# Scatters of routed rows moved ahead of the second pair's normalisation factors on GpSimd

## The chip, the cores and the metric

One core of a Trainium2 chip runs the whole kernel. The metric is the device time of one execution in microseconds. A core has five engines with a queue each: PE (TensorE), DVE (VectorE), ACT (ScalarE), POOL (GpSimd) and SP (SyncE, which here only issues DMAs). Each engine works through its queue in order and waits on semaphores that the others raise.

## The reference

128 batches of 128 tokens with 256 features go through cross attention and then a routed feed-forward layer with 32 experts:

```python
x = x + xattn(layernorm(x), ctx, Wq, bq, Wk, bk, Wv, bv, Wo, bo)      # 16 heads of 16, softmax over 128 keys
# ffn, on layernorm(x):
logits = x_flat @ router_w.T + router_b
routed_idx = jnp.argmax(logits, axis=-1)
h = jax.nn.relu(x_flat @ w1 + b1)          # for each expert, 64 hidden
y = jax.nn.relu(h @ w2 + b2)
out_flat = y_all[routed_idx, jnp.arange(n)]  # each token takes its own expert
x = x + ffn
```

## The kernel before

A block is four batches (512 tokens); there are 32 blocks. The work is a software pipeline written out by hand: each engine has a loop over iterations s and, but for POOL, over the four batches u of block s, and each engine's order in the loop is its order on the chip. In iteration s the attention of block s runs, and beside it the projections of block s+1 and s+2, the second layer norm and the router's logits of block s-1, the choice and the ranks of block s-2, and the scatter of block s-3.

The steps that matter below:

- PE, batch u: the scores `sc` (L786), two transposes of a pair of normalised batches into `pA` (L748; in u = 0 and 1 of xn, in u = 2 and 3 of xn2), the transpose of the maxima (L779), attend of the batch before (L804, into `pB`), the subtraction of the maxima (L795), the scores for the next maxima (L773), a projection (L757), the values V (L764), and the output projection (L811). The scores of a batch wait for the copy of V of the batch before, and the transposes for the copy of the projection before.
- DVE, batch u: maxima (L574), residual (L583, which writes x2 into `row`), the copy mxT (L588), `xnT` (L593, in u = 0 and 1), then for the batch before `tr` (L598, behind attend), `inv`, `nrm` (L602), `aT`; then maxima again. In u = 0 also slot_sum (L637), in u = 1 best and choose (L614 to L626).
- ACT, batch u: the copy xnT (L441) or xn2T (L446), norm1 or norm2 (L428), the squares (L436), four exponentials (L452), the copy of V (L456), and the copy of the projection (L463 or, masked, twice L466).
- POOL, iteration s: rstd2(s-1, 0), place(s-3), rstd1(s+2), split(s+2), rstd2(s-1, 1), scatter(s-3), add_bo(s+1), meta(s-2), fresh_pages(s-2).

rstd2(q, h) makes the factors of the second layer norm for batches 2h and 2h+1 of block q with six operations on 128x2 values (L282 to L292); it waits for the squares of batch 2h+1, and norm2 of batch 2h waits for it. split (L306, L308) divides the context of a block into a high and a low part. scatter casts the four slots of each token to integers (L370) and issues four indirect DMAs (L374), one for a batch, which write 128 rows of 260 words each to the pages of their experts in HBM. It waits for the slots (slot_out), for the pages to have been filled, for the scatters of the block before, and for the token numbers (meta_out). add_bo (L298) adds the output bias to the x of the next block. SP loads x and a part of the context and fills a page behind each residual.

When all rows are scattered, SP loads the pages group by group, PE, ACT and DVE run each page through its expert, and POOL scatters the results to the output (L403).

Of the kernel before, what the change touches and what calls it, by code (L numbers as in the profile page):

```python
# [53 lines left out]
def build(nc, x, ctxT, wq, wk, wv, wo, bq, bk, bv, bo, wr, rb, w1, w2, consts, out):  # L54
# [14 lines left out]
    with ctx:  # L69
# [88 lines left out]
        def after(eng, name, per, q, k):  # L158
            eng.wait_ge(S[name], q * per + k + 1)
# [3 lines left out]
        def live(q):  # L163
            return 0 <= q < NQ
# [87 lines left out]
        def _(pool):  # L252
# [41 lines left out]
            def add_bo(q):  # L294
                if q == 0:
                    pool.wait_ge(S["bo_out"], 1)
                after(pool, "xn_out", 2, q, 1)
                pool.tensor_tensor(xs[:, q % 4], xs[:, q % 4], bo_s[:, :].unsqueeze(1).to_broadcast([P, QB, D]),  # L298
                                   ALU.add).then_inc(S["xb_out"], 1)

            def split(q):
                for c in range(2):
                    pool.wait_ge(S[f"ld_c{c}"], q * 16 + 16)
                if q >= 2:
                    after(pool, "V_done", 4, q - 2, 3)
                pool.tensor_copy(cHi[:, q % 2], cT[:, :, :]).then_inc(S["ctx_hi"], 1)  # L306
                after(pool, "ctx_hi", 1, q, 0)
                pool.tensor_tensor(cLo[:, q % 2], cT[:, :, :], cHi[:, q % 2].bitcast(F32), ALU.subtract).then_inc(S["ctx_out"], 1)  # L308
# [72 lines left out]
            for s in range(-1, NQ + 3):  # L381
                if live(s - 1):
                    rstd2(s - 1, 0)
                if live(s - 3):
                    place(s - 3)
                if live(s + 2):
                    rstd1(s + 2)
                if s >= 0 and live(s + 2):
                    split(s + 2)
                if live(s - 1):  # L390
                    rstd2(s - 1, 1)
                if live(s - 3):
                    scatter(s - 3)
                if live(s + 1):
                    add_bo(s + 1)
                if live(s - 2):
                    meta(s - 2)
                    fresh_pages(s - 2)
# [633 lines left out]
```

## Time and profile before

| | us |
|---|---|
| median of 3 runs | 1323.57 |
| lowest, highest | 1322.7, 1328.38 |
| the profiled execution | 1323.38 |
| its span, first to last instruction | 1321.3 |

Over the span PE is busy 87%, DVE 71%, POOL 65%, ACT 63%. Attention with its blocks reaches from the start to about 1016 us, the last choice and scatters to 1048, the pages to the end. In all tables a row of a timeline has the start in us from the span's start, the duration in us, the engine, the line, the operation, the tiles and their shape, a count where several in a row are merged, and in brackets how long the engine was idle before it and who released it. A start and a duration together give the end.

### The profile page before, as it was taken

Reading aid. Unit: us, or ns where it says so; the run is one execution under the profiler, and the core shown is the slowest. Engines: PE = TensorE matmul, PEld = TensorE weight load, DVE = VectorE, ACT = ScalarE, POOL = GpSimd, SP = SyncE. Lnnn points to the kernel's source line nnn. Section 1 sums busy time; section 2 is a strip of 40 time slices with the busy share of each in tenths; the row PEclk is TensorE's granted clock in tenths of the full one; section 3 lists DMA queues with packets and bytes.
Section 4 is the critical chain, followed back from the end, with each engine's and each line's share of the span. In section 5 each row is a group of like instructions: output and inputs, shape, how many; then the busy total and the mean of one; then the engine's idle time right before and its main releaser. Section 6 shows DMA issues by size and latency. Waiting matters only on the chain.

```text
span 1321.3 us, 38981 instructions
## 1 busy us (share of the span) xinstructions
PE 1146.4 (87%) x15015; PEld 877.5 (66%) x15015; DVE 941.1 (71%) x2449; ACT 832.5 (63%) x1892; POOL 854.2 (65%) x1613
## 2 busy tenths in 40 slices
PE   5999999999999999999999999999986087777775
PEld 4777777777777777777777777777764076666664
DVE  3788887788787888888778878788774155555554
ACT  3677776777777777777677777777763044444443
POOL 4535767767667777677776766777555656666555
PEclk8999999999999999999999999999998599999999
DMA  8315223422222222222222222221102245555540
GB/s 253 108 51 116 78 68 99 120 75 66 74 67 65 71 69 66 71 78 70 76 83 67 67 74 67 66 74 54 34 23 92 93 139 177 173 166 167 153 113 19
DMA packets 89235, 120.37 MB, mean 91 GB/s; under 512 B 12176, under 2 KB 71963, under 8 KB 88861
## 3 DMA queue, kind: packets, MB, share of 16 engines
q1 hardware_dynamic: 75230, 84.03, 22.5%
q0 software_dynamic: 13824, 33.85, 7.0%
q8 instruction: 122, 2.00, 0.7%
q14 instruction: 59, 0.48, 0.1%
HBM read 60.61 MB, written 59.31 MB: 91 GB/s over the span
## 4 chain that ended last, share of the span: by engine, by line
PE 53%; DVE 31%; issue 6%; ACT 4%; POOL 2%; DMA 1%; another core or an unknown queue 1%; DVEq 1%; SPq 0%; POOLq 0%; ACTq 0%
DVE mx L574 14%; PE pB L804 11%; PE pA L757 8%; PE pB L811 5%; PE sc L965 4%; PE sc L764 4%; PE m L973 3%; DVE tr L598 3%; PE sc L956 3%; PE sc L786 3%; DVE nrm L602 3%; PE m L773 3%; DVE row L583 3%; PE sc L795 2%; PE pA L748 2%
## 5 line engine op out<-in xcount | busy, mean ns | idle before, releaser
L574 DVE TENSOR_REDUCE mx<-m 128x4 bf16<-128x512 f32 x512 | 324.0, 673 | 53.3 <-PE m L773 53.0
L452 ACT ACTIVATE arena<-sc 128x512 f32<-128x512 f32 x512 | 264.5, 603 | 37.0 <-PE sc L795 23.1
L403 POOL DMA_INDIRECT out<-arena x160 | 159.7, 998 | 108.7 <-DVE arena L722 71.3
L786 PE MATMUL sc<-qk 32*128 32x256 f32 x2048 | 167.5, 397 | 0.3
L374 POOL DMA_INDIRECT pages<-row,slot_i x128 | 132.1, 1032 | 49.2 <-issue 32.2
L804 PE MATMUL pB<-arena 128*32 128x128 f32 x4096 | 147.7, 277 | 13.6 <-DVE row L583 0.5
L598 DVE STREAM_TRANSPOSE tr<-pB 128x512 f32<-128x512 f32 x128 | 91.8, 718 | 84.7 <-PE pB L804 74.2
L533 ACT ACTIVATE arena<-sc 128x256 f32<-128x256 f32 x160 | 61.3, 383 | 137.2 <-PE sc L956 87.2
L811 PE MATMUL pB<-wo_s,aT 128*128 128x256 f32 x512 | 138.6, 393 | 4.4 <-DVE aT L607 4.4
L804 PEld LDWEIGHTS pB<-arena 128*32 128x32 f32 x4096 | 108.6, 110 | 36.2 <-DVE row L583 30.9
L786 PEld LDWEIGHTS sc<-qk 32*128 32x128 f32 x2048 | 115.5, 186 | 0.7 <-ACT arena L456 0.6
L282 POOL TENSOR_SCALAR row<-row 128x2 f32<-128x2 f32 x64 | 14.6, 228 | 156.6 <-ACT xn L436 156.6
L773 PE MATMUL m<-qk 32*128 32x128 bf16 x2048 | 103.2, 217 | 2.8 <-ACT qk L466 1.8
L757 PE MATMUL pA<-cHi,wqkv 128*128 128x512 f32 x252 | 96.9, 425 | 9.4 <-DVE wqkv L641 9.4
L757 PE MATMUL pA<-xnT,wqkv 128*128 128x512 f32 x372 | 103.5, 414 | 0.0
L446 ACT ACTIVATE xn2T<-pA 128x512 f32<-128x512 f32 x64 | 38.2, 597 | 103.6 <-remote 61.7
L965 PE MATMUL sc<-arena,cT 128*128 128x128 f32 x640 | 101.0, 282 | 0.0
L811 PEld LDWEIGHTS pB<-wo_s,aT 128*128 128x128 f32 x512 | 87.6, 190 | 18.3 <-issue 5.9
L764 PE MATMUL sc<-wqkv,cHi 128*128 128x256 f32 x512 | 97.9, 284 | 0.5 <-ACT arena L452 0.5
L764 PEld LDWEIGHTS sc<-wqkv,cHi 128*128 128x128 f32 x512 | 87.9, 190 | 11.4 <-ACT arena L452 0.6
L973 PE MATMUL m<-w2s,arena 128*128 x160 | 53.8, 419 | 46.8 <-ACT arena L537 33.1
L773 PEld LDWEIGHTS m<-qk 32*128 32x128 bf16 x2048 | 63.1, 93 | 46.3 <-issue 32.3
(145 smaller groups left out, 2717.4 us busy)
## 6 DMA issues: line engine op xcount, KB each, us to landing
arena<-pages SPq DMA_DIRECT2D x40, 520.0 KB
cT<-ctxT SPq DMA_DIRECT2D x64, 256.0 KB, 4.2
xs<-x_in SPq DMA_DIRECT2D x128, 128.0 KB, 2.1
pages<-empty SPq DMA_DIRECT2D x120, 130.0 KB, 3.0
pages<-empty SPq DMA_DIRECT2D x1, 5200.0 KB, 19.3
out<-arena POOLq DMA_INDIRECT x160
w2s<-w SPq DMA_DIRECT2D x1, 2080.0 KB
qk<-w SPq DMA_DIRECT2D x1, 2064.0 KB
```

The source lines that it names most:

```text
L374: pool.indirect_dma_start(pages, bass.IndirectOffsetOnAxis(slot_i[:, u:u + 1], 0), row[:, q % 4, u, :], None, bounds_check=last_slot, oob_ ...
L403: pool.indirect_dma_start(out_rows, bass.IndirectOffsetOnAxis(pr[:, r, COL_TOKEN:COL_TOKEN + 1].bitcast(U32), 0), pr[:, r, 0:D], None, bou ...
L452: act.activation(pt[:, u % 2, g].rearrange("p i k -> p (i k)"), sc[g][:, :], ACT.Exp).then_inc(S["exp_out"], 1)
L574: ins = dve.tensor_reduce(mx[:, 32 * g:32 * g + 4], mb[i][:, :].rearrange("p (h k) -> p h k", h=4), AX.X, ALU.max)
L598: dve.transpose(tr[:, :], pB[:, :]).then_inc(S["tr_out"], 1)
L757: ins = pe.matmul(proj_bank(q, n)[:, :], wqkv[:, w, a, i, c * P:(c + 1) * P], src[:, i, :], start=(i == 0 and (a, b) == HI_LO[0]), stop=(i ...
L764: ins = pe.matmul(sc[0][:, 0:D], (cHi, cLo)[a][:, q % 2, i, u * P:(u + 1) * P], wqkv[:, 2, b, i, :], start=(i == 0 and (a, b) == HI_LO[0]) ...
L773: ins = pe.matmul(mb[i][:, j * P:(j + 1) * P], qMh[rows, q % 2, m, c, u * P:(u + 1) * P], kTh[rows, q % 2, c, u * P:(u + 1) * P], start=Tr ...
L786: pe.matmul(dst, kT[rows, q % 2, c, u * P:(u + 1) * P], qM[rows, q % 2, :, c, u * P:(u + 1) * P], start=(c == 0), stop=False, skip_group_c ...
L804: ins = pe.matmul(pB[32 * g:32 * g + 32, j * P:(j + 1) * P], vs[:, q % 2, u, h, :], pt[:, u % 2, g, j, :], start=True, stop=True)
L811: ins = pe.matmul(pB[:, 0:D], aT[:, i, :], wo_s[:, i, :], start=(i == 0), stop=(i == 1))
L965: ins = pe.matmul(sc[2 + n % 2][:, 0:P], w1p[:, n % W1R, i * HID:i * HID + P], pnT[:, n % DEEP, i * P:(i + 1) * P], start=(i == 0), stop=( ...
```

## The change

In POOL's loop scatter(s-3) now stands ahead of rstd2(s-1, 1), directly behind split(s+2).

```diff
                 if s >= 0 and live(s + 2):
                     split(s + 2)
+                if live(s - 3):
+                    scatter(s - 3)
                 if live(s - 1):
                     rstd2(s - 1, 1)
-                if live(s - 3):
-                    scatter(s - 3)
                 if live(s + 1):
                     add_bo(s + 1)
```

PE, DVE, ACT and SP have the same instructions in the same order. POOL has the same instructions. In the middle of the run, POOL's queue stood so, from the split to add_bo; what is in brackets is what a row waits for:

```order
L308 TENSOR_TENSOR cLo<-cT,cHi 128x1024 [waits ctx_hi]
L282 TENSOR_SCALAR row<-row 128x2 [waits sq_out]
L283 TENSOR_SCALAR row<-row 128x2
L285 TENSOR_TENSOR sq<-row 128x2 [waits mean2_out]
L288 TENSOR_TENSOR row<-row,sq 128x2 [waits eps2_out,sq2_out]
L290 TENSOR_TENSOR row<-row,half 128x2 [waits var2_out]
L292 TENSOR_TENSOR row<-row 128x2 [waits pow2_out]
L370 CAST slot_i<-slot 128x4 [waits slot_out,scattered,fill0]
L374 DMA pages<-row,slot_i 20480x260 [waits meta_out,slot_int]
L374 DMA pages<-row,slot_i 20480x260 x3
L298 TENSOR_TENSOR xs<-xs,bo_s 128x1024 [waits xn_out]
```

At the same place it now reads:

```order
L308 TENSOR_TENSOR cLo<-cT,cHi 128x1024 [waits ctx_hi]
L370 CAST slot_i<-slot 128x4 [waits slot_out,scattered,fill0]
L374 DMA pages<-row,slot_i 20480x260 [waits meta_out,slot_int]
L374 DMA pages<-row,slot_i 20480x260 x3
L282 TENSOR_SCALAR row<-row 128x2 [waits sq_out]
L283 TENSOR_SCALAR row<-row 128x2
L285 TENSOR_TENSOR sq<-row 128x2 [waits mean2_out]
L288 TENSOR_TENSOR row<-row,sq 128x2 [waits eps2_out,sq2_out]
L290 TENSOR_TENSOR row<-row,half 128x2 [waits var2_out]
L292 TENSOR_TENSOR row<-row 128x2 [waits pow2_out]
L298 TENSOR_TENSOR xs<-xs,bo_s 128x1024 [waits xn_out]
```

The cast and the four scatters have passed the six operations of rstd2, whose wait for the squares (sq_out) now stands behind them.

In iteration 32 there is no split and no add_bo. On POOL, from the end of place to meta, it was:

```order
L360 TENSOR_TENSOR nxt<-nxt,shift_d 128x32 [waits nxt_old,shift_out]
L282 TENSOR_SCALAR row<-row 128x2 [waits sq_out]
L283 TENSOR_SCALAR row<-row 128x2
L285 TENSOR_TENSOR sq<-row 128x2 [waits mean2_out]
L288 TENSOR_TENSOR row<-row,sq 128x2 [waits eps2_out,sq2_out]
L290 TENSOR_TENSOR row<-row,half 128x2 [waits var2_out]
L292 TENSOR_TENSOR row<-row 128x2 [waits pow2_out]
L370 CAST slot_i<-slot 128x4 [waits slot_out,scattered,fill1]
L374 DMA pages<-row,slot_i 20480x260 [waits meta_out,slot_int]
L374 DMA pages<-row,slot_i 20480x260 x3
L315 TENSOR_SCALAR expert<-idx 128x4 [waits idx_out]
```

And it now is:

```order
L360 TENSOR_TENSOR nxt<-nxt,shift_d 128x32 [waits nxt_old,shift_out]
L370 CAST slot_i<-slot 128x4 [waits slot_out,scattered,fill1]
L374 DMA pages<-row,slot_i 20480x260 [waits meta_out,slot_int]
L374 DMA pages<-row,slot_i 20480x260 x3
L282 TENSOR_SCALAR row<-row 128x2 [waits sq_out]
L283 TENSOR_SCALAR row<-row 128x2
L285 TENSOR_TENSOR sq<-row 128x2 [waits mean2_out]
L288 TENSOR_TENSOR row<-row,sq 128x2 [waits eps2_out,sq2_out]
L290 TENSOR_TENSOR row<-row,half 128x2 [waits var2_out]
L292 TENSOR_TENSOR row<-row 128x2 [waits pow2_out]
L315 TENSOR_SCALAR expert<-idx 128x4 [waits idx_out]
```

The scatters stand directly behind place here, and rstd2 of the last block behind them.

## Rows read from the trace of the kernel before

**Rows 1.** The page's chain of work that ended last, share by engine.

```profile
PE 53%; DVE 31%; issue 6%; ACT 4%; POOL 2%; DMA 1%; another core or an unknown queue 1%; DVEq 1%; SPq 0%; POOLq 0%; ACTq 0%
```

**Rows 2.** Waits (total us, times, longest), and L602 (ns min/median/max).

```profile
POOL row L282 <- ACT xn L436: 156.6, 64, 9.5
...
ACT xn2T L446 <- remote: 61.7, 23, 2.7
...
L602 DVE TENSOR_TENSOR nrm<-tr,inv x128: 424/441/1610, 43.7 to 1012.6; 128x256 f32<-128x256 f32 x128
```

**Rows 3.** Timeline of POOL in block 19 and at the start of block 20's factors.

```profile
617.60 2.37 POOL L308 TENSOR_TENSOR cLo<-cT,cHi 128x1024 fp32r<-128x1024 f32 x1
622.36 0.23 POOL L282 TENSOR_SCALAR row<-row 128x2 f32<-128x2 f32 x1 [2.40 <-ACT xn L436]
...
624.27 0.20 POOL L292 TENSOR_TENSOR row<-row 128x2 f32<-128x2 f32 x1
...
625.11 1.13 POOL L374 DMA_INDIRECT pages<-row,slot_i  x1 [0.51 <-POOL slot_i L370]
...
630.19 2.40 POOL L298 TENSOR_TENSOR xs<-xs,bo_s 128x1024 f32<-128x1024 f32 x1
...
652.97 0.23 POOL L282 TENSOR_SCALAR row<-row 128x2 f32<-128x2 f32 x1 [2.21 <-ACT xn L436]
```

**Rows 4.** Timeline of DVE in batches 1 and 2 of block 19.

```profile
622.13 0.72 DVE L598 STREAM_TRANSPOSE tr<-pB 128x512 f32<-128x512 f32 x1
...
627.87 0.41 DVE L583 SCALAR_TENSOR_TENSOR row<-pB,xs 128x256 f32<-128x256 f32 x1
...
629.38 0.22 DVE L588 COPY mxT<-m 128x128 bf16<-128x128 bf16 x1 [1.09 <-PE m L779]
631.04 0.72 DVE L598 STREAM_TRANSPOSE tr<-pB 128x512 f32<-128x512 f32 x1 [1.44 <-PE pB L804]
...
632.08 0.80 DVE L602 TENSOR_TENSOR nrm<-tr,inv 128x256 f32<-128x256 f32 x1
```

**Rows 5.** Timeline of ACT in the same stretch.

```profile
624.95 0.38 ACT L456 ACTIVATE arena<-sc 128x256 f32<-128x256 f32 x1 [0.47 <-PE sc L764]
625.23 1.44 ACT L466 ACTIVATE qk<-pA,bqm,cst 128x512 f32<-128x512 f32 x2
629.34 0.60 ACT L446 ACTIVATE xn2T<-pA 128x512 f32<-128x512 f32 x1 [2.67 <-remote]
629.84 0.59 ACT L428 ACTIVATE xn<-row 128x256 f32<-128x256 f32 x1
```

**Rows 6.** Timeline of PE in the same stretch.

```profile
620.98 1.08 PE L804 MATMUL pB<-arena 128*32 128x128 f32 x32
...
626.96 0.66 PE L748 MATMUL pA<-cst,xn 128*128 128x128 f32 x4
...
628.34 1.40 PE L804 MATMUL pB<-arena 128*32 128x128 f32 x32
```

**Rows 7.** DVE's copy mxT of batch 0 in blocks 1 and 2.

```profile
62.79 0.23 DVE L588 COPY mxT<-m 128x128 bf16<-128x128 bf16 x1
...
91.77 0.23 DVE L588 COPY mxT<-m 128x128 bf16<-128x128 bf16 x1
```

**Rows 8.** Timelines of POOL, PE and DVE in batch 2 of block 4.

```profile
165.89 1.13 POOL L374 DMA_INDIRECT pages<-row,slot_i  x1 [0.83 <-POOL slot_i L370]
...
168.79 1.08 PE L804 MATMUL pB<-arena 128*32 128x128 f32 x32
...
171.81 0.72 DVE L598 STREAM_TRANSPOSE tr<-pB 128x512 f32<-128x512 f32 x1 [2.15 <-remote]
```

**Rows 9.** Timelines of DVE and POOL in iteration 32.

```profile
1013.45 0.24 DVE L637 TENSOR_REDUCE slot<-t 128x4 f32<-128x128 f32 x1
...
1015.81 0.31 POOL L282 TENSOR_SCALAR row<-row 128x2 f32<-128x2 f32 x1 [3.85 <-ACT xn L436]
...
1022.70 0.97 POOL L374 DMA_INDIRECT pages<-row,slot_i  x1 [0.30 <-issue]
```

## The prediction

> **What bounds the kernel now.** I read the chain of work first: PE has 53% of it, DVE 31%, POOL 2% [rows 1]. POOL is no engine on which time is lost directly, so four scatters begun earlier, or six tiny operations begun later, are worth nothing by themselves. The question is what they do to PE, DVE and ACT. Next I read the waits of the whole run [rows 2]. POOL's largest is the first operation of rstd2 (L282) behind ACT's squares, 156.6 us in 64 times: that is the gap the change fills. Another is odd: ACT's xn2T copy waited 23 times, 61.7 us in total, for a releaser that the trace can't name (`remote`). To see what lies behind it I opened one steady block, 613.9 to 644.5 us; its period is 30.61 us (622.36 to 652.97, the same instruction one block on) [rows 3].
>
> In that block the scatters start at 625.11 (call this t0), and add_bo behind the fourth at 630.19 [rows 3]. What PE finishes in this time is signalled late. The transposes of xn2 start at 626.96 and take 0.66, so they end at 627.62 [rows 6], but ACT's copy of them starts only at 629.34, after 2.67 idle [rows 5]. DVE is done with the residual at 628.28 and should copy mxT at once; it does so at 629.38 [rows 4]. Attend (L804) starts at 628.34, takes 1.40 where batch 1's took 1.08 [rows 6], and `tr` behind it starts at 631.04 [rows 4]. So there are two holds: completions due at t0+2.5 come out at t0+4.2, and those due at t0+4.6 at t0+5.9. In batch 1, with no scatter running, `tr` starts at 622.13 without idle, 0.07 after attend's end at 622.06 [rows 4, 6]. DVE's `nrm` (L602) then takes 0.80, where its median is 0.44, beside add_bo's last 0.5 us [rows 2 to 4].
>
> I take the holds to belong to the scatters: they recur at the same distance in the steady blocks, and the one block with batches in full swing and no routing work ran in 28.98 us (62.79 to 91.77) [rows 7]. What inside the chip joins a scatter to PE's signals no row says.
>
> **What the change does, part by part.** The instructions and their counts are the same; only POOL's order moves.
>
> 1. The scatters. cLo ends at 619.97. From rstd2's end (624.47) to t0 was 0.64, so t0 becomes 619.97 + 0.64 = 620.61, 4.5 us earlier [rows 3]. slot_out, the one late input, is DVE's slot_sum just behind batch 0, so it isn't late. Carried along, the holds cover 623.1 to 624.8 and (from 625.2 at the latest) to 626.5. DVE works in that time without needing PE: after `tr` at 622.13 [rows 4] come the maxima, best and choose, and the residual at 627.87, whose input PE makes soon behind V. ACT needs V at 624.95 and then runs the two masked projections from 625.23 to 626.67, and had 2.67 idle behind them [rows 5].
>    The doubtful completion is that of V, due about 624.9, t0+4.3. If it is let through, ACT loses nothing, mxT follows at 628.28, attend runs 628.34 to 629.42 and `tr` starts at 629.45, 1.59 earlier. `nrm` loses its extra 0.36 too, since add_bo is over by then. Both together are 1.95, but a block that is otherwise free took 28.98, so I cap the gain at 30.61 - 28.98 = 1.6. If V is caught in the second hold, it comes at t0+5.93 = 626.54; the copy and the projections end 0.28 + 1.44 later, at 628.3; the transposes start 0.29 behind (as 626.96 behind 626.67) and take 0.66, to 629.2; attend ends 1.1 later, and `tr` starts at 630.35, 0.7 earlier. For being caught speaks block 4: scatters from 165.89, attend ended at 169.87, t0+3.98, and `tr` started only at 171.81, t0+5.92 [rows 8]. Against it: the first hold lets go at t0+4.2, just before V is due. The rows are equally near to both, so I take the middle, 1.15 per block.
> 2. rstd2's second half (the factors of batches 2 and 3). It took 622.36 to 624.47, 2.11. It now stands behind the four scatters, 5.08 from t0 to add_bo [rows 3]: 625.7 to 627.8. Who waits is ACT's norm2 of batch 2, which stands behind the xn2T copy. Freed of its hold that copy starts at 627.65, and norm2 0.5 later, 628.15 (as 629.84 behind 629.34 [rows 5]). The margin is 0.35, and behind norm2 stand only the squares before the exponentials, which cannot start before attend's end at 629.42 and the subtraction behind it; two ACT steps of 0.5 lie between, so the real margin is about 0.5 to 1.0. Cost: nothing, between 0 and 0.5 per block if the scatters are slowed by more than that margin.
> 3. add_bo and meta. add_bo starts at 627.8 instead of 630.19; the expert is chosen before the residual at 627.87, and POOL then waits for the ranks as before. It may slow the residual at 627.87, which reads one operand of SBUF: at most the 0.36 that `nrm` loses now. I take 0, and the cap of 1.6 covers it.
> 4. Loads. SP issues x, fill and half of the context behind the residual, at 621 as at 628. All four scatters now run beside the earlier set instead of two beside the later. No engine waited for these loads in the steady block; the cost by itself is 0, but it can lengthen the holds (rival C).
> 5. The end. In iteration 32 POOL idled 3.85 before rstd2 at 1015.81, though the slots were summed at 1013.69 [rows 9]. The scatters now fill that from 1013.8. By the steady block's lengths, 0.7 + 5.08 + 2.27, rstd2 ends at 1021.85 instead of the scatters' end at 1023.70: 1.9 earlier, on the path, since POOL alone leads from there to the pages.
>
> The sum: 29 blocks (3 to 31) scatter beside attention. 29 x 1.15 = 33.4, and 1.9 at the end: 35.3. The profiled execution took 1323.38 (span 1321.3 and 2.1 around it), practically the median 1323.57, so no correction: 1323.4 - 35.3 = **1288**. Its own range, from 0.7 to 1.6 per block, is 1301 to 1275.
>
> The Trainium skill bears on this against me. "SBUF — State Buffer", section "Who interferes with whom", says that only the port pair shared by VectorE and GpSimd causes contention and that TensorE waits for nobody there. The trace agrees for `nrm` beside add_bo (0.80 us against a median of 0.44). For PE it shows late completions beside the scatters, which that rule doesn't give; if the rule is the whole story, the holds belong to something else and rival B is what happens.
>
> **The rivals.**
> B, the holds stay where they are, since they belong to batch 2 of a block (its PE work or SP's loads behind it) and not to the scatters. For: I infer the link from position, and no row names a releaser. Against: the loads are issued behind every second batch, but PE is late only here. Then only `nrm` is freed, at most 29 x 0.36 = 10, and the end, 1.9: 1311 to 1321.
> C, **slower**: the holds begin earlier than the rows of before can show, because the first scatter now meets batch 1's attend. That attend is due at 622.06, t0+1.45, and DVE takes it up with no slack. If it is held as the first group is, to t0+4.2 = 624.8, DVE loses 2.7; less the 1.6 that goes away, that is 1.1 per block, 32 in all, less 1.9: 1353. It decides from where a completion at t0+1.45 is caught. Against: no wait in the rows shows a completion held that was due before t0+2.5. For: before, nothing on which an engine waited fell due between 1.0 and 2.5, so the rows are silent there, and the loads are now at hand.
> D, the price is paid in other coin: longer holds, scatters slowed by DVE's SBUF work, norm2 late. With 0.7 to 1.2 per block of it little is left: 1316 to 1332.
> E, the change doesn't do what it says: slot_out or the previous scatters hold slot_i back. Slots are summed in batch 0 and the last scatters were issued a block before, so I give this nothing of its own.
>
> **How the numbers follow.** Forecast (1275 to 1301) 0.50; B 0.15; C 0.14; D 0.16; better than 1275 0.05. Within 0.5% (6.6 us, about what a measurement of this kernel can tell from no change) are 1317 to 1330. Faster: 0.50 + 0.05 + two thirds of B (0.10) = 0.65. Same: the rest of B and most of D, 0.18. Slower: C and the tail of D, 0.17. The range of 8 in 10 leaves out C and a little at the low end: 1272 to 1332.
>
> **What would show it.** Scatters at 4.5 us before their present distance to the block's start; ACT's `remote` wait for xn2T gone or under 15 us in total; DVE's mxT copy following the residual within 0.1, and `tr` some 1.0 behind it instead of 1.44 behind a late start; a period of 29.0 to 29.9. V's copy on ACT starting at once means the upper gain, 1.6 us late the lower. Wrong would be: a wait before batch 1's `tr` (C), the same waits at batch 2 (B), norm2 waiting for POOL (D).

## The result, and the profile after

The changed kernel takes 1419.19 us (median of 4 runs, 1413.83 to 1427.14) against 1324.78 us of the kernel before (4 runs, 1322.7 to 1328.38). The ratio is 1.069, with a 95% interval from 1.064 to 1.074: the change makes the kernel 7% slower, where 3% faster was forecast. The profiled execution took 1421.39 us, its span 1418.3.

A hold, in what follows, is a completion of TensorE (the semaphore update by which it tells the others that a result is there) that comes late. First, where in the program the time went. These two groups hold all of a block's scatters and all copies `mxT`; the numbers behind the counts are the shortest, the median and the longest in ns, then the starts of the first and the last in us. Before:

```profile
L374 POOL DMA_INDIRECT pages<-row,slot_i x128: 971/982/1251, 134.9 to 1046.7; - x128
L588 DVE COPY mxT<-m x128: 223/225/226, 35.9 to 1005.7; 128x128 bf16<-128x128 bf16 x128
```

After:

```profile
L374 POOL DMA_INDIRECT pages<-row,slot_i x128: 971/976/1255, 129.6 to 1146.4; - x128
L588 DVE COPY mxT<-m x128: 224/225/226, 35.4 to 1107.0; 128x128 bf16<-128x128 bf16 x128
```

The last copy `mxT` comes 101.3 us later, so the whole loss lies in the attention blocks. From that copy to the last scatter it is 39.4 us instead of 41.0, the only place where the change did what it was meant to do; the pages behind take 2.7 less, which no run explains.

To see in which batch the time goes I take the starts of `mxT`, of which every batch has one. Over the blocks 4 to 29, a block (from one batch 0 to the next) takes 30.62 us before and 34.29 after. By batches:

| us, mean of blocks 4 to 29 | 0 to 1 | 1 to 2 | 2 to 3 | 3 to next | block |
|---|---|---|---|---|---|
| before | 6.98 | 8.45 | 7.56 | 7.63 | 30.62 |
| after | 6.98 | 11.72 | 7.99 | 7.60 | 34.29 |

The step from batch 1 to batch 2 is where the scatters now lie. The page's line of the chain that ended last, and the longest waits of the run that are new or have grown (total us, times, longest; the first was 34.7 us before, the last 9.8):

```profile
PE 52%; DVE 26%; issue 8%; another core or an unknown queue 5%; ACT 3%; POOL 2%; DVEq 1%; DMA 1%; SPq 0%; POOLq 0%; ACTq 0%
```

```profile
POOL need L327 <- ACT rks L484: 192.1, 31, 8.7
ACT arena L452 <- remote: 105.6, 28, 4.0
...
DVE tr L598 <- remote: 72.9, 22, 4.1
```

Before, 1% of the chain was put down to an unknown releaser [rows 1]; now it is 5%. ACT's xn2T wait for `remote` [rows 2] is gone, as forecast. In its place ACT waits for it 28 times ahead of the exponentials (L452), 3.8 us each time, and DVE 22 times ahead of `tr`, 3.3 us each.

Block 19 again, in the same stretch as [rows 3 to 6]. It now starts at 672.8. POOL, the first and the fourth scatter and the bias:

```profile
679.28 1.14 POOL L374 DMA_INDIRECT pages<-row,slot_i  x1 [0.29 <-POOL slot_i L370]
...
683.28 0.97 POOL L374 DMA_INDIRECT pages<-row,slot_i  x1 [0.30 <-issue]
...
686.32 2.38 POOL L298 TENSOR_TENSOR xs<-xs,bo_s 128x1024 f32<-128x1024 f32 x1
```

PE and ACT (attend of batch 1, the scores for the next maxima, the projection, the exponentials):

```profile
679.87 1.08 PE L804 MATMUL pB<-arena 128*32 128x128 f32 x32
...
682.07 0.30 PE L773 MATMUL m<-qk 32*128 32x128 bf16 x4 [0.48 <-issue]
...
683.02 1.64 PE L757 MATMUL pA<-xnT,wqkv 128*128 128x512 f32 x6
```

```profile
685.13 2.06 ACT L452 ACTIVATE arena<-sc 128x512 f32<-128x512 f32 x4 [3.96 <-remote]
```

DVE:

```profile
684.35 0.72 DVE L598 STREAM_TRANSPOSE tr<-pB 128x512 f32<-128x512 f32 x1 [3.34 <-remote]
...
687.70 1.14 DVE L615 TENSOR_TENSOR eq<-lg,top 128x128 f32<-128x128 f32 x1
...
691.35 0.23 DVE L588 COPY mxT<-m 128x128 bf16<-128x128 bf16 x1
692.57 0.72 DVE L598 STREAM_TRANSPOSE tr<-pB 128x512 f32<-128x512 f32 x1 [0.99 <-PE pB L804]
```

Call the first scatter's start t0, 679.28. Attend ends at 680.95, t0+1.67, but `tr` starts only at t0+5.07; the exponentials start at t0+5.85. Batch 2 is now undisturbed: `mxT` follows the residual at once and `tr` 1.22 after it, as forecast. So the holds did move with the scatters, and at their new place they catch attend and the subtraction of the maxima, on which both DVE and ACT wait. PE goes on to its next work meanwhile, but slowly: the projection starts 3.15 behind attend's start, where it was 1.56 in the kernel before. Since the ends of matmuls in a trace are modelled, the rows don't say whether a late completion was sent late or came late.

From `tr` to `mxT` DVE then works almost without a break (0.24 us idle on average over the 26 blocks), so it is `tr`, and what DVE meets behind it, that make the step from batch 1 to 2. The exponentials' wait is beside that path.

And DVE meets something: there is a second loss in these rows. DVE's comparison `eq` (L615) takes 1.14 beside POOL's bias, add_bo (L298), which now directly follows the factors. Over the run, before:

```profile
L615 DVE TENSOR_TENSOR eq<-lg,top x32: 291/293/1474, 103.3 to 1030.1; 128x128 f32<-128x128 f32 x32
```

After:

```profile
L615 DVE TENSOR_TENSOR eq<-lg,top x32: 291/1440/2180, 102.8 to 1129.8; 128x128 f32<-128x128 f32 x32
```

The two are tied. `eq` ends when add_bo does, 0.14 behind it in block 19. In the 26 blocks `tr` starts anywhere from t0+4.3 to 5.8; where it starts early `eq` takes 2.0 us, where it starts late 0.64, and the step stays between 11.5 and 11.8. So in the changed kernel the end of add_bo fixes the step, and DVE meets add_bo only because the hold has made it late.

And a third. The step from batch 2 to 3 takes 7.25 us in 14 of the 26 blocks, as in block 19, and 8.6 to 10.2 in the others, as in block 18. These are stretches of the trace after (stretch, length, PE busy and instructions, granted clock, DMA share, GB/s), the first two of block 18 and the last two of block 19:

```profile
652.50:656.20 3.70, 2.00 (x30) 1.00 0.00 0
656.20:658.70 2.50, 2.39 (x55) 0.65 0.34 107
...
687.50:691.10 3.60, 2.04 (x30) 1.00 0.00 0
691.10:693.60 2.50, 2.39 (x60) 1.00 0.38 110
```

PE, standing behind `eq` and the maxima, was busy for 2.00 of 3.70 us, and then the granted clock was 0.65 for a while (a mixture of the two levels, 2.4 and 1.2 GHz); in block 19, after nearly the same pause, it stayed at 1.00. A fall costs 1.5 us in most of these blocks. The kernel before shows no lowered clock in its blocks 4 to 29.

### The profile page after: what moved, and what is told of

Read it like the earlier page. It is cut to its first block, busy times and chain, and to the rows that moved or that the text cites. A ratio compares the mean times of both kernels' runs of the same rounds, so it can differ in the third digit from the quotient of the medians.

```text
span 1418.3 us, 38981 instructions
## 1 busy us (share of the span) xinstructions
PE 1174.7 (83%) x15015; PEld 887.1 (63%) x15015; DVE 963.3 (68%) x2449; ACT 830.2 (59%) x1892; POOL 855.9 (60%) x1613
## 3 DMA queue, kind: packets, MB, share of 16 engines
q0 software_dynamic: 13824, 33.85, 6.5%
## 4 chain that ended last, share of the span: by engine, by line
PE 52%; DVE 26%; issue 8%; another core or an unknown queue 5%; ACT 3%; POOL 2%; DVEq 1%; DMA 1%; SPq 0%; POOLq 0%; ACTq 0%
PE pA L757 11%; DVE mx L574 11%; PE pB L804 8%; PE pB L811 7%; PE sc L764 5%; PE m L773 4%; PE sc L965 3%; DVE eq L615 3%; PE sc L795 3%; PE m L973 3%; PE sc L786 2%; DVE row L583 2%; PE sc L956 2%; DVE tr L598 2%
## 5 line engine op out<-in xcount | busy, mean ns | idle before, releaser
L452 ACT ACTIVATE arena<-sc 128x512 f32<-128x512 f32 x512 | 264.6, 603 | 159.8 <-remote 105.6
L773 PE MATMUL m<-qk 32*128 32x128 bf16 x2048 | 115.8, 221 | 27.6 <-issue 24.2
L533 ACT ACTIVATE arena<-sc 128x256 f32<-128x256 f32 x160 | 61.2, 382 | 130.8 <-PE sc L956 76.4
L764 PE MATMUL sc<-wqkv,cHi 128*128 128x256 f32 x512 | 102.7, 294 | 28.3 <-ACT arena L452 27.7
L327 POOL TENSOR_TENSOR need<-rks,room 128x32 f32<-128x32 f32 x32 | 8.1, 253 | 192.1 <-ACT rks L484 192.1
L773 PEld LDWEIGHTS m<-qk 32*128 32x128 bf16 x2048 | 68.9, 95 | 79.4 <-issue 65.9
L757 PE MATMUL pA<-xnT,wqkv 128*128 128x512 f32 x372 | 113.7, 444 | 0.0
L456 ACT ACTIVATE arena<-sc 128x256 f32<-128x256 f32 x128 | 50.0, 390 | 71.4 <-PE sc L764 71.4
```

Of the source, the lines that this page charges most:

```text
L452: act.activation(pt[:, u % 2, g].rearrange("p i k -> p (i k)"), sc[g][:, :], ACT.Exp).then_inc(S["exp_out"], 1)
L757: ins = pe.matmul(proj_bank(q, n)[:, :], wqkv[:, w, a, i, c * P:(c + 1) * P], src[:, i, :], start=(i == 0 and (a, b) == HI_LO[0]), stop=(i ...
L764: ins = pe.matmul(sc[0][:, 0:D], (cHi, cLo)[a][:, q % 2, i, u * P:(u + 1) * P], wqkv[:, 2, b, i, :], start=(i == 0 and (a, b) == HI_LO[0]) ...
L773: ins = pe.matmul(mb[i][:, j * P:(j + 1) * P], qMh[rows, q % 2, m, c, u * P:(u + 1) * P], kTh[rows, q % 2, c, u * P:(u + 1) * P], start=Tr ...
```

## The experiments

e1 to e5 leave out rows, so only their blocks, measured as above, can be compared; the others do all the work and are compared by the time of the whole run too. "Before" is the kernel before on the same chip beside the run. Where no interval is given, there was one run. The steps are means of one trace.

| run | us | before | ratio (95%) | 1 to 2 | 2 to 3 | block |
|---|---|---|---|---|---|---|
| e1, before, no scatters | 1293.5 | 1311.1 | | 8.86 | 7.41 | 30.86 |
| e2, after, no scatters | 1290.6 | 1311.1 | | 8.51 | 7.60 | 30.69 |
| e3, after, rows skipped | 1266.1 | 1311.1 | | 7.37 | 7.25 | 29.23 |
| e4, after, one scatter | 1298.0 | 1311.1 | | 8.66 | 7.54 | 30.78 |
| e5, after, two scatters | 1318.7 | 1328.0 | | 8.98 | 7.25 | 30.82 |
| e6, after, scatters wait | 1318.9 | 1328.0 | | 8.09 | 7.81 | 30.51 |
| e7, before, behind the bias | 1421.3 | 1328.0 | | 8.52 | 10.96 | 34.09 |
| e8, scatters apart | 1416.9 | 1328.0 | 1.067 (1.064 to 1.071) | 10.38 | 8.92 | 34.13 |
| e9, after, loads wait | 1446.4 | 1318.7 | 1.096 (1.094 to 1.099) | 11.75 | 8.94 | 35.30 |
| e10, before, loads wait | 1318.6 | 1318.7 | 0.999 (0.998 to 1.000) | 8.45 | 7.67 | 30.73 |
| e11, apart, bias late | 1293.8 | 1318.7 | 0.981 (0.978 to 0.983) | 7.36 | 7.61 | 29.74 |
| e12, after, bias late | 1359.0 | 1321.1 | 1.028 (1.025 to 1.032) | 10.33 | 7.24 | 32.16 |
| e13, all apart | 1276.9 | 1321.1 | 0.968 (0.965 to 0.972) | 7.36 | 7.24 | 29.19 |
| e14, first one early, apart | 1290.5 | 1321.1 | 0.977 (0.974 to 0.981) | 7.35 | 7.60 | 29.72 |

### e1 to e4: is it the scatters, and what of them?

e1 and e2 take the scatters out of the kernel before and of the changed one; a store to a spare word counts for them.

```
-                for u in range(QB):
+                for u in range(0):
...
+                pool.memset(gone[:, :], 0.0).then_inc(S["scattered"], 64)
```

> The kernel before with its 128 scatters to the pages left out; a memset of one column raises their semaphore, so no routed row is written and the pages hold only the fill. Theory 1 (a run of scatters holds back PE's completions, and that is what both kernels pay): the holds in batch 2 vanish, the period falls from 30.6 to about 29.0 us, and with the tail shorter by three groups of scatters (some 15 us) the time is about 1265. Rival (the holds belong to batch 2 of a block, its loads or PE's own work): the period stays at 30.6 or falls only by 0.4, time about 1300 to 1310.

> The changed kernel with the scatters left out in the same way. Theory 1: its order costs nothing by itself, so it takes what the run before it takes within 5 us. Rival (the later factors or add_bo beside other work of DVE cost the time): it stays well above that run, by up to the 95 us that the change cost, and DVE's or ACT's waits of the changed kernel in batch 1 are still there.

e3 keeps the four instructions but gives them slots beyond the last page:

```
-                pool.tensor_copy(slot_i[:, :], slot[:, :]).then_inc(S["slot_int"], 1)
+                pool.tensor_scalar(slot_i[:, :], slot[:, :], 1048576.0, None, ALU.add).then_inc(S["slot_int"], 1)
```

> The changed kernel with slots beyond the end of the pages, so that POOL still makes all four scatters but their rows are out of bounds and none is written. If making the scatter on POOL is what holds PE back, the holds and the 1419 us stay. If the moving of the rows is (512 rows of 1040 bytes per block), the holds go and the time is about that of the changed kernel without scatters plus the length of POOL's tail, some 1285.

e4 issues one of the four, at the first one's place (`range(1)` for `range(QB)`, and the counts waited for to match).

> The changed kernel with one of the four scatters of a block (rows of batches 1 to 3 are not scattered), at the place of the first. If each scatter holds PE for a time of its own, the attend of batch 1, due 1.67 us behind the scatter's start, is still held, by 1 to 2 us, and the period is 30 to 31 us. If only scatters in a run do it (a second one begun while the first moves its rows), nothing is held and the period is about 29.0.

In e1, e2 and e4 no engine waits ahead of batch 1's `tr`, yet they gain nothing over before in the step 1 to 2. The reason is `eq`, 1.78, 1.44 and 1.59 us long on average in blocks 4 to 29, here in e1 (POOL's add_bo is at L299 and `eq` at L617 there):

```profile
622.59 2.36 POOL L299 TENSOR_TENSOR xs<-xs,bo_s 128x1024 f32<-128x1024 f32 x1
```

```profile
623.32 1.78 DVE L617 TENSOR_TENSOR eq<-lg,top 128x128 f32<-128x128 f32 x1
```

Without scatters between the factors and add_bo, add_bo runs beside `eq`, and `eq` lasts until 0.15 us behind add_bo's end. No expectation had that, so the 29.0 us a block of e1 and e4 did not come; that e2 would be within 5 us of e1 did. e3 has the scatters' time on POOL, so that add_bo comes at 604.57, behind `eq`; all holds are gone as well, and with 29.23 us a block and 1266 us in all it is faster than the 1285 expected. The page's line of the queue, and DVE in block 19:

```profile
q0 software_dynamic: 13824, 0.17, 0.7%
```

```profile
598.77 0.72 DVE L598 STREAM_TRANSPOSE tr<-pB 128x512 f32<-128x512 f32 x1
...
602.11 0.29 DVE L615 TENSOR_TENSOR eq<-lg,top 128x128 f32<-128x128 f32 x1
```

The queue shows as many packets as before, but 0.17 MB for 33.85, and in block 19 `tr` starts without idle. POOL's scatter instructions are there, about as long as before, and hold nothing, so the hold needs rows that are really written. That it is the moving itself is not shown: in e13, below, a hold is over before the first packet of its rows. And `eq` takes 0.29 in each of the 26 blocks: with the changed order and no hold, DVE is past `eq` before add_bo starts.

29.2 us is what a block takes when nothing disturbs it; the kernel before is 1.4 above that. e4 has a single scatter and no hold; it is the block's first one, and the experiments below show that this matters.

### e5: two scatters

As e4, with two of the four.

> The changed kernel with the first two of a block's four scatters only; half of the routed rows are therefore never written, and only the attention blocks can be compared (changed kernel 34.3 us a block there, with one scatter 30.8, with none 30.7). Theory 1, the rows in flight hold back the completions of TensorE, and the more the longer: one scatter of 128 rows holds nothing for long, four hold attend's completion for 3.4 us; two should hold it for about half of that, 1 to 1.7 us, so 31.5 to 32.5 us a block. Theory 2, there is a threshold on what the queue can hold: two are either as harmless as one (30.8) or as bad as four (34.3). Theory 3, it is the first scatter's place beside attend that matters and one scatter was enough of it: 30.8.

`tr` and the exponentials of batch 1; the first scatter is at 622.89:

```profile
625.81 0.72 DVE L598 STREAM_TRANSPOSE tr<-pB 128x512 f32<-128x512 f32 x1 [1.19 <-PE pB L804]
```

```profile
625.89 2.07 ACT L452 ACTIVATE arena<-sc 128x512 f32<-128x512 f32 x4 [1.11 <-PE sc L795]
```

Both are let go at t0+2.9 to 3.0. With one there was no wait, with four `tr` came at t0+5.07. The hold grows with the number of scatters in the run. The block's time hides it: 30.82 us is what the second and third theory said, because `eq`, met later, is shorter here (0.73 on average where e4 has 1.59). By the rows it is the first theory's hold of 1 to 1.7.

### e6 and e7: the four together at two other places

e6 adds a wait ahead of the scatters of the changed order:

```
                 if live(s - 3):
+                    if live(s - 1):
+                        after(pool, "sq_out", 4, s - 1, 3)
                     scatter(s - 3)
```

> The changed kernel's order on GpSimd, all four scatters, but the first waits until ScalarE has squared batch 3, some 2.3 us later than in the changed kernel and some 2 us earlier than in the kernel before. The hold should move with it. Theory 1, what is held is whatever TensorE completes while the rows are moved: attend of batch 1 would then post before the rows (no wait of 3.3 us ahead of tr in that batch) and the wait moves to the next completions, as score maxima or projection; a block of 31.5 to 33.5 us, since GpSimd's own later work (factors, residual bias) comes 2.3 us later too. Theory 2, the changed order itself costs (factors behind the scatters, bias beside the eq comparison) and not the time of the rows: 34.3 us or more.

e7 puts them one place later than before:

```
                 if live(s - 1):
                     rstd2(s - 1, 1)
+                if live(s + 1):
+                    add_bo(s + 1)
                 if live(s - 3):
                     scatter(s - 3)
-                if live(s + 1):
-                    add_bo(s + 1)
```

> The kernel before with the four scatters moved one place the other way, behind the addition of the residual bias (2.4 us later). Nothing is left out. Theory 1, the holds move 2.4 us later: the two of the kernel before (ahead of tr and of the copy of maxima in batch 2) go, and others come at attend and maxima of the end of batch 2 or of batch 3; the block stays between 30 and 34 us according to where DVE waits. Also the bias, now straight behind the factors, runs beside the eq comparison, as in the runs without scatters, and costs some 1.2 us in batch 1. Theory 2, only an earlier place is harmful: 30.6 plus that 1.2 us.

e6 begins the scatters at 619.37 in block 19, 9.1 into the block (6.5 after, 11.2 before), and costs no more than the kernel before; its block is shorter than either theory said. ACT's xn2T copy is held until 625.26, t0+5.9, but DVE waits little. Its `nrm` at 626.88 took 2.23, beside add_bo. In e7 the hold lies on attend and subtraction again, of batch 2 this time, with t0 at 680.53:

```profile
686.28 0.72 DVE L598 STREAM_TRANSPOSE tr<-pB 128x512 f32<-128x512 f32 x1 [3.36 <-remote]
```

```profile
686.36 2.06 ACT L452 ACTIVATE arena<-sc 128x512 f32<-128x512 f32 x4 [3.11 <-remote]
```

They come at t0+5.75 and t0+5.83. The block is nearly as long as the changed kernel's, but that is chance. Against an undisturbed block (e13), e7 loses 1.16 us in the step 1 to 2, again with `eq` beside add_bo (1.46 us), and 3.72 in the step 2 to 3. There `tr` starts 2.4 later behind `mxT`, and the other 1.3 come behind it, in a step in which the granted clock is lower in all 26 blocks (0.69 on average). In block 19 (PE, PEld, DVE, ACT and POOL busy, granted clock, DMA share, GB/s):

```profile
682.68:693.70 11.02, 10.17 (x109) 7.70 (x109) 5.73 (x17) 5.19 (x12) 5.35 (x14) 0.69 0.29 86
```

So earlier or later is not the point: moved 4.7 us ahead (the change) or 2.1 behind (e7), the hold of the four catches an attend and the subtraction near its start; at the two places between (e6 and the kernel before) it catches them near its end or not at all.

### e8: one at a time

The scatters are issued singly: behind the factors, the bias, the expert's work and the list of fresh pages.

`scatter` is split into the making of `slot_i` and `scatter_one(q, us)`, which issues those of the batches us. Against the kernel before:

```
                 if live(s - 3):
                     scatter(s - 3)
+                if live(s - 3):
+                    scatter_one(s - 3, (0,))
                 if live(s + 1):
                     add_bo(s + 1)
+                if live(s - 3):
+                    scatter_one(s - 3, (1,))
                 if live(s - 2):
                     meta(s - 2)
+                if live(s - 3):
+                    scatter_one(s - 3, (2,))
...
```

> Nothing is left out. The four scatters of a block are issued one at a time, between the factors, the bias, the expert's work and the list of fresh pages, so that at least 2 us lie between two of them. Theory 1, one scatter alone holds nothing that is waited for (the run with one of four: 30.8 us a block against 30.7 without any), and only a run of them does: 29.5 to 30.8 us a block, 1290 to 1320 us in all against 1324.8 of the kernel before. Theory 2, what counts is the number of rows and not their spacing: each scatter holds a completion for about 1 us, four times a block, 31 to 34 us a block, 1330 to 1420 us.

By its time this seemed to speak for "each scatter costs by its rows". The rows say otherwise: of batch 1's and 2's `tr` none waits longer than the 0.99 that it waits in an undisturbed block. Batch 3's does, behind the fourth scatter, which begins 9.6 us behind the third:

```profile
693.80 1.08 POOL L376 DMA_INDIRECT pages<-row,slot_i  x1 [0.17 <-issue]
...
695.24 0.72 DVE L609 STREAM_TRANSPOSE tr<-pB 128x512 f32<-128x512 f32 x1 [1.46 <-PE pB L815]
```

Attend's matmuls end at 694.67, 0.87 behind the scatter's start, and `tr` starts 0.57 later. So a scatter by itself can hold PE too, for half a microsecond here; the step from batch 3 to the next takes 7.85 us (7.79 in e11 and e14, which have their fourth scatter there as well) instead of 7.61. The great loss is another one. What went wrong is `eq`, with add_bo next behind a scatter:

```profile
678.61 1.12 POOL L376 DMA_INDIRECT pages<-row,slot_i  x1 [0.51 <-POOL slot_i L370]
679.77 2.35 POOL L298 TENSOR_TENSOR xs<-xs,bo_s 128x1024 f32<-128x1024 f32 x1
```

```profile
678.99 3.29 DVE L626 TENSOR_TENSOR eq<-lg,top 128x128 f32<-128x128 f32 x1
```

PE then stood, and its clock fell (same columns as above):

```profile
681.10:684.50 3.40, 0.02 (x1) 1.00 0.11 39
...
686.50:689.50 3.00, 3.00 (x12) 0.50 0.56 167
```

These two steps take 19.3 us (10.38 + 8.92), 4.7 more than e3's 14.6. 3.0 of them are `eq`; most of the rest is the clock: the six projections that come next, first in e8, then in e3, where the clock stayed up:

```profile
686.55 2.93 PE L768 MATMUL pA<-xnT,wqkv 128*128 128x512 f32 x6
```

```profile
599.19 1.66 PE L757 MATMUL pA<-xnT,wqkv 128*128 128x512 f32 x6
```

### e9 and e10: are SyncE's loads part of it?

In the changed kernel three loads (x, a fill, half a context) are issued 0.6 to 1.4 us behind the first scatter. e9 makes them wait until the scatters have landed:

```
+                    if u == 3 and q >= 2:
+                        sp.wait_ge(S["scattered"], 64 * (q - 1))
                     if live(q + 4):
                         load_x(q + 4, u)
```

> The changed kernel, nothing left out; only SyncE's loads that fell among the scatters (fourth rows of x, one page fill, half a context; issued 0.6 to 1.4 us after the first scatter's start) now wait until the block's scatters have landed. Theory 1, the rows of the scatters and those loads share the DMA engines, and it is the two together that hold TensorE's completions for 3.4 us: with the loads gone the hold is 1 to 2 us long, as the first one of the kernel before (1.7 us, no load near it), and a block takes 31.5 to 32.5 us instead of 34.3. Theory 2, the rows alone do it, whatever else is moved: 34 us or more.

e10 does the same to the loads behind batch 0's residual in the kernel before (`u == 0 and q >= 3`, `64 * (q - 2)`).

> The kernel before, nothing left out; the loads that SyncE issues at the scatters' end (first rows of x, one fill, half a context; 3.2 to 4.1 us after the first scatter's start) wait until the block's scatters have landed. Theory 1 (rows and loads together hold): the second hold, 1.3 us ahead of tr in batch 2, goes, 0.8 to 1.3 us less a block, 1290 to 1305 us in all; the first one, with no load near it, stays. Theory 2 (rows alone): both stay, 1320 to 1330 us.

The holds stay in both, so the loads are not their cause. In e9, t0 at 692.28:

```profile
696.59 0.72 DVE L600 STREAM_TRANSPOSE tr<-pB 128x512 f32<-128x512 f32 x1 [2.59 <-remote]
...
699.93 2.18 DVE L617 TENSOR_TENSOR eq<-lg,top 128x128 f32<-128x128 f32 x1
...
704.61 0.23 DVE L590 COPY mxT<-m 128x128 bf16<-128x128 bf16 x1
```

But in the changed kernel they lengthen the hold. Over the blocks 4 to 29 `tr` starts at t0+4.22 on average instead of t0+5.05, and the exponentials at t0+5.09 instead of 5.83 (block 19, with t0+5.8, is one of four of the 26 in which they come as late as that). The first theory was right in that, though not in its 1 to 2 us. It gains nothing, because `eq` starts sooner behind add_bo's start (699.60) and lasts 2.18 in most blocks, 0.83 longer than in the changed kernel: just what `tr` had won. That e9 is slower still, by 1.0 us a block, comes from the clock, which falls more often (8.94 in the step 2 to 3 instead of 7.99). In e10 nothing changes: `tr` of batch 2 still waits 1.42 us.

### e11, e13, e14: apart, with the bias out of the way

e11 is e8 with the expert's work (which waits for `idx`, made from `eq`) ahead of add_bo, and a wait ahead of the third scatter. Against the kernel before:

```
                 if live(s - 3):
                     scatter(s - 3)
+                    scatter_one(s - 3, (0,))
+                if live(s - 2):
+                    meta(s - 2)
                 if live(s + 1):
                     add_bo(s + 1)
+                if live(s - 3):
+                    scatter_one(s - 3, (1,))
+                    if live(s):
+                        after(pool, "sq_out", 4, s, 0)
+                    scatter_one(s - 3, (2,))
                 if live(s - 2):
-                    meta(s - 2)
                     fresh_pages(s - 2)
+                if live(s - 3):
+                    scatter_one(s - 3, (3,))
```

> Nothing left out. The scatters of a block one at a time again, but the residual bias is no longer next behind the first of them: it comes behind the expert's work, which waits for the comparison (eq) that the bias held up for 3.0 us in the run before; the third scatter also waits for ScalarE's square of batch 0. Theory 1 (single scatters hold nothing; the 34.1 us a block of the run with them apart came from the bias holding eq, and from the lower granted clock after TensorE had stood): eq takes 0.3 us again, 29.3 to 30.6 us a block, 1285 to 1320 us in all. Theory 2 (each scatter costs by its rows): over 31.5 us a block, over 1345 us.

1293.8 us: faster than before by 1.7 to 2.2%. `eq` is 0.29 in block 19. The second and third scatter are still 1.39 apart, and the maxima of that time wait for a releaser that the trace can't name:

```profile
616.55 1.09 POOL L376 DMA_INDIRECT pages<-row,slot_i  x1 [0.17 <-issue]
617.94 0.98 POOL L376 DMA_INDIRECT pages<-row,slot_i  x1 [0.30 <-issue]
```

```profile
618.61 1.29 DVE L585 TENSOR_REDUCE mx<-m 128x4 bf16<-128x512 f32 x2 [0.42 <-remote]
```

e13 parts those two as well, with `after(pool, "max_out", 8, s, 7)` for the wait on `sq_out`.

> Nothing left out. As the run with the scatters apart and the bias late (29.7 us a block), but the third scatter waits for the last maxima of batch 3, so that it no longer follows 1.4 us behind the second; that pair held score maxima's completion for 1.9 us. Theory 1 (only scatters that follow one another within some 1.4 us hold anything): the two holds behind the pair go, 29.2 to 29.6 us a block, 1275 to 1292 us. Theory 2 (each scatter's rows hold what comes meanwhile): a hold appears wherever the third scatter goes, 29.7 us a block or more, 1294 us or more.

```profile
600.84 1.13 POOL L376 DMA_INDIRECT pages<-row,slot_i  x1 [0.51 <-POOL slot_i L370]
...
605.53 1.09 POOL L376 DMA_INDIRECT pages<-row,slot_i  x1 [0.17 <-issue]
611.17 0.99 POOL L376 DMA_INDIRECT pages<-row,slot_i  x1 [4.56 <-DVE mx L585]
615.18 1.08 POOL L376 DMA_INDIRECT pages<-row,slot_i  x1 [0.16 <-issue]
```

With at least 4 us from one to the next, a block takes 29.19 us, as much as in e3, which moves no rows. 1276.9 us is 3.2% faster than before and the best version found: the same scatters with the same rows, apart and at these places, cost nothing.

That is not the same as holding nothing. The trace also keeps the moment of each semaphore's update. In block 19 PE's scores for the next maxima end at 605.71, 0.18 behind the second scatter's start, and their update comes at 606.85, 1.14 late. It is so in all 26 blocks; completions due 0.6 behind the fourth scatter come 0.67 late, and attend, due 1.2 behind the third, 0.25. DVE and ACT are busy with earlier work just then, so almost nothing waits. The second scatter's first row packet starts only at 607.24, behind the hold. Nothing is late behind a block's first scatter, in e13 (due 0.7 and 1.0 behind it) or in e4 (0.4, 0.5 and 1.7). Why the first differs stays open.

e14 is e11 with the first scatter alone at the place that the change gave to all four.

> Nothing left out. As the run with the scatters apart and the bias late, with the first scatter alone moved ahead of the second pair's factors, to the place that the change gave it, 1.5 us ahead of attend's end. Theory 1 (it is the run of four that was harmful, not the early place): no wait ahead of tr in batch 1, 29.5 to 30.0 us a block, 1285 to 1300 us. Theory 2 (a scatter ahead of attend holds it): a wait of 1 us or more ahead of tr in batch 1, 30.7 us a block or more, over 1315 us.

```profile
606.62 1.13 POOL L376 DMA_INDIRECT pages<-row,slot_i  x1 [0.29 <-POOL slot_i L370]
```

```profile
608.16 0.72 DVE L609 STREAM_TRANSPOSE tr<-pB 128x512 f32<-128x512 f32 x1
```

`tr` starts without idle, 1.54 behind the scatter's start. The early place is harmless for the block's first scatter alone; the run of four was not. Whether one of the other three would be harmless there no run shows.

### e12: the change without the collision

The changed kernel, its four scatters in a run where the change puts them, with only add_bo moved behind the expert's work:

```
+                if live(s - 2):
+                    meta(s - 2)
                 if live(s + 1):
                     add_bo(s + 1)
                 if live(s - 2):
-                    meta(s - 2)
                     fresh_pages(s - 2)
```

> The changed kernel, nothing left out, with the residual bias behind the expert's work instead of ahead of it; that work waits for VectorE's eq comparison, so the bias can no longer run beside it (eq took 1.1 us in the profiled block of the changed kernel, 0.3 us in the kernel before). The four scatters stay where the changed kernel has them. Theory 1 (the hold costs 3.3 to 3.4 us ahead of tr in batch 1, the bias beside eq the rest): eq is 0.3 us again, 33.2 to 33.6 us a block, 1385 to 1400 us in all. Theory 2 (most of the loss is the changed order of the bias): under 32 us a block, under 1360 us.

```profile
649.59 0.72 DVE L599 STREAM_TRANSPOSE tr<-pB 128x512 f32<-128x512 f32 x1 [3.26 <-remote]
...
652.93 0.29 DVE L616 TENSOR_TENSOR eq<-lg,top 128x128 f32<-128x128 f32 x1
```

In this block the hold is as long as in the changed kernel, and yet the kernel takes 60 us less. The second theory's numbers are the nearer ones (1359.0 is just under its 1360, 32.16 us a block just over its 32); for the first I had reckoned with `eq`'s own 0.85 us only, and not with what follows from it.

The loss can now be split, per block. Undisturbed, a block takes 29.19 (e13). The kernel before pays 30.62 - 29.19 = 1.43 for its holds in batch 2; the change gives that back. The hold at attend costs 32.16 - 29.19 = 2.97 (e12). With add_bo beside `eq` it is 11.72 - 10.33 = 1.39 more in the step 1 to 2, 1.06 of it `eq`'s own lengthening and 0.33 a hold that lasts longer than e12's (`tr` at t0+5.05 on average against t0+4.73), and 7.99 - 7.24 = 0.75 more in the next step, where the clock falls in about half of the blocks; e12, with `eq` short, has 7.24 throughout. -1.43 + 2.97 + 1.39 + 0.75 = 3.68, against 34.29 - 30.62 = 3.67 measured. The terms are differences between the same four kernels, so that they add up tests nothing. And the last two are no loss of the new order by itself: e3 has that order and no hold, and pays neither.

## Why the prediction was wrong

**Step 1, the scatters.** Right were the distance (the scatters begin 4.7 us earlier in their block; 4.5 was said), that the holds belong to the scatters and move with them (so rival B is out), that batch 2 would be clean, and what that gives back, 1.43 (the kernel before against e13) within the forecast 0.7 to 1.6. Wrong was the window: "the holds cover 623.1 to 624.8". That start, t0+2.5, was only the first held completion in the rows of before. Nothing on which an engine waited fell due just ahead of it, and I read the silence as freedom. In the changed kernel attend of batch 1, due at t0+1.67, is held, and `tr` starts at t0+5.05 on average, behind 3.3 us of idle; by e12 that costs 2.97 us a block. This is rival C, which named place and reason and got 0.14; its own argument, that the rows are silent between t0+1.0 and 2.5, should have made it an even chance. Its price was nearly right for what it described: 1353 us, where the hold alone (e12) gives 1359. C rightly followed `tr`. It let it go at t0+4.2, like the first group of before; without the loads (e9) it goes at t0+4.22, and with them 0.8 later. What C did not follow is where DVE goes from `tr`.

**Step 3, the bias.** "I take 0" holds as long as step 1 does: in e3, with the same order on POOL and no hold, `eq` is over before add_bo starts and takes 0.29. It fell with step 1. The hold brings DVE to `eq` 3.3 us later, into add_bo, and what follows is 1.39 + 0.75 = 2.1 us a block, some 60 us in all, nearly everything that C missed. No rival put a hold and add_bo together, though the working had `nrm` beside add_bo at 0.80 instead of 0.44 [rows 2 to 4] in hand. The Trainium skill, "SBUF — State Buffer", section "Who interferes with whom", states that a VectorE instruction with two SBUF inputs contends with a GpSimd instruction that reads SBUF, and that the second to issue is fully blocked until the first is done. The trace agrees on the blocking (`eq` 1.78 us in e1, until 0.15 after add_bo's end), but not always on the order: in e8, by the rows, `eq` started 0.78 before add_bo and was blocked all the same, and there the measurement decides. So the price of C should have listed every such instruction that a late DVE has in the 2.4 us of add_bo's new place: `eq` and what choose does behind it. The same section's rule that only that port pair causes contention does not give the waits behind PE, which move with the scatters all the same: there the measurement decides.

**Steps 2 and 4.** The factors came later and nobody waited for them in the steady blocks (ACT's norm2 waits for POOL twice in the whole run, 7.0 us in all). The loads make the hold 0.8 us longer in the changed kernel (e9), as step 4 allowed, and do nothing in the kernel before (e10); taking them away gained nothing.

**Step 5, the end.** 1.9 us were said, 1.6 came.

**Rival D** named longer holds and other coin, but priced them at 1.2 us a block at most. Its range does not follow from that either: 1288 and 29 x 0.7 to 1.2 are 1308 to 1323, not 1316 to 1332. The last thing missed was the clock: no step asked what a pause of PE would set off.

## What to carry to other kernels

Indirect scatters belong singly between other work, and not where an engine is about to wait for TensorE: four in a run held up its completions for up to 4 us, the same four at least 4 us apart cost nothing at the places of e13 and 0.2 us a block where the fourth stood beside attend (e8, e11). Before GpSimd's elementwise work is moved, list VectorE's instructions with two SBUF inputs at its new place, also for the case that VectorE comes late; with a longer hold and the clock's fall, add_bo beside one comparison of 0.3 us came to 2.1 us a block. And where a trace shows a disturbance only from some point on, ask whether anything was due earlier that could have shown it.

## What the runs showed of the hardware

- While several indirect scatters in close succession are issued and their rows written, completions of TensorE reach the engines late. Two hold until t0+2.9 to 3.0 (e5). Behind four, waiting engines are let go at t0+4.2 and 5.9 in block 19 of the kernel before, and in the 26 blocks of the changed kernel `tr` at about t0+4.3 (6 blocks), 5.05 (14) or 5.75 (6), without the loads at 4.2 (25 of 26). TensorE's own next work comes later too: the projection 3.15 behind attend's start instead of 1.56. With the same instructions and their rows skipped (e3) nothing is held.
- A scatter at least 4 us behind the last one holds too, but briefly: completions due 0.2, 0.6 and 0.9 us behind its start came at 1.3 to 1.4 (e13's second and fourth, e8's fourth). Behind the first scatter of a block nothing was late (e4, e13, e14). In e13 the hold ends 0.4 before the scatter's first row packet starts, so what in the chip joins the two stays open.
- Time since t0 is not the whole rule for what is caught: in e6, ACT took V up at 621.26, t0+1.9, without delay, where the changed kernel's attend at t0+1.67 was held.
- add_bo that stands directly behind a scatter on GpSimd blocked a two-input VectorE instruction which, by the rows, had started 0.78 us before add_bo did (e8: `eq` at 678.99, add_bo at 679.77, `eq` ended at 682.28). In the kernel before, with a second scatter behind the first, `eq` at the same distance took 0.29. By the rows the blocking begins while the scatter still runs.
- TensorE busy for 2.00 of 3.70 us in one stretch was followed by a granted clock of 0.65; standing for 3.4 us, by 0.50. It came in 12 of 26 blocks of the changed kernel and not in others with nearly the same pause.
